# Soft stage of a graph network with a slice attention, x in triples: the row norm moved from VectorE to ScalarE, two tiles ahead, in eight slots

## The reference

```python
# graph part: x = x + MLP(layernorm(x), sums of the edge rows by their target row)
aggr = segment_sum(edge_features, edge_index[1], num_segments=6250)
h = relu(concat([layernorm(x), aggr]) @ W1 + b1)
x = x + relu(h @ W2 + b2) @ W3 + b3
# slice attention on the normed rows, 8 heads of 64, 64 slices each
xn = layernorm(x)
fx_mid, x_mid = heads(xn @ W_fx + b_fx), heads(xn @ W_x + b_x)
slice_weights = softmax((x_mid @ W_slice + b_slice) / clip(temperature, 0.1, 5), axis=-1)
slice_token = einsum('bhnc,bhng->bhgc', fx_mid, slice_weights) / (slice_weights.sum(rows) + 1e-5)
q, k, v = slice_token @ W_q, slice_token @ W_k, slice_token @ W_v
out_slice = softmax(q @ k.T / 8) @ v
x = x + (einsum of out_slice with slice_weights) @ W_out + b_out
```

## Time and profile before

| | us |
|---|---|
| median of 3 timed runs | 646.18 (644.64 to 648.68) |
| profiled execution, its own time | 645.15 |
| span of the profiled execution | 643.4 |
| PE busy | 600.5 (93%) |
| DVE busy | 389.9 (61%) |
| ACT busy | 281.8 (44%) |
| POOL busy | 231.3 (36%) |
| granted TensorE clock, mean | 0.991 |

### The profile page before, as it was taken

The page is one execution under the profiler, slowest core; times in us unless marked ns, Lnnn a source line. Parts: engine busy times, 40 slices in busy tenths (PEclk is TensorE's granted clock), DMA queues, the critical chain, the costliest instruction groups (busy, mean ns, idle before and its releaser), DMA issues.

```text
span 643.4 us, 11467 instructions
## 1 busy us (share of the span) xinstructions
PE 600.5 (93%) x3433; PEld 355.1 (55%) x3433; DVE 389.9 (61%) x1089; ACT 281.8 (44%) x400; POOL 231.3 (36%) x283
## 2 busy tenths in 40 slices
PE   5679999979998999999899899999999998999997
PEld 2345555544554555454489344444444444888885
DVE  6745545335576566655458888888888887322221
ACT  5145655612221222222120444555455546777772
POOL 4345565500000000000123666666666665595000
PEclk9799999989999999999999999999999999999999
DMA  8999999999999999996120134333343334011112
GB/s 296 380 396 397 408 409 408 373 350 386 366 361 384 377 353 369 385 362 251 41 81 1 33 66 77 70 65 65 68 77 68 65 66 81 25 73 73 73 73 81
DMA packets 104841, 134.01 MB, mean 208 GB/s; under 512 B 57339, under 2 KB 59345, under 8 KB 104805
## 3 DMA queue, kind: packets, MB, share of 16 engines
q1 hardware_dynamic: 103989, 133.29, 61.3%
q10 hardware_dynamic: 816, 0.26, 0.2%
HBM read 114.29 MB, written 6.40 MB: 188 GB/s over the span
## 4 chain that ended last, share of the span: by engine, by line
PE 74%; DMA 21%; DVE 2%; SPq 1%; issue 1%; ACT 0%; DVEq 0%
DMA ring_mem<-edge_attr_in 18%; PE ps L1583 13%; PE ps L1491 13%; PE ps L1515 13%; PE ps L1235 10%; PE ps L1356 7%; PE ps L1277 6%; PE ps L1271 5%; DMA x_sb<-x_in 3%; PE ps L1476 2%; PE ps L1266 2%; PE ps L1348 1%; SPq L404 1%; DVE ring_mem L1105 0%; DVE ring_mem L1107 0%
## 5 line engine op out<-in xcount | busy, mean ns | idle before, releaser
L969 DVE TENSOR_TENSOR big<-big,ps 128x64 f32 x319 | 70.6, 221 | 103.8 <-PE ps L1266 60.3
L1235 PE MATMUL ps<-ring_mem,side 128*32 128x256 f32 (+1 forms) x1596 | 103.2, 394 | 26.2 <-DMA ring_mem<-edge_attr_in 24.9
L1491 PE MATMUL ps<-ring_mem,xn 128*128 128x512 f32 x196 | 93.4, 599 | 1.0 <-DVE ring_mem L1119 0.7
L1515 PE MATMUL ps<-side,ring_mem 128*128 128x512 f32 x196 | 92.3, 593 | 1.9 <-ACT ring_mem L744 1.9
L1235 PEld LDWEIGHTS ps<-ring_mem,side 128*32 128x32 f32 (+1 forms) x1596 | 50.9, 112 | 63.9 <-issue 32.1
L1583 PE MATMUL ps<-side,ring_mem 128*128 128x256 f32 x360 | 77.9, 379 | 0.0
L640 POOL TENSOR_TENSOR ring_mem<-ring_mem 128x512 f32<-128x512 f32 x48 | 66.1, 1376 | 30.0 <-DVE ring_mem L1119 30.0
L1583 PEld LDWEIGHTS ps<-side,ring_mem 128*128 128x128 f32 x360 | 68.4, 190 | 9.3
L759 ACT ACTIVATE ring_mem<-ring_mem 128x512 f32<-128x512 f32 x49 | 30.9, 630 | 90.5 <-POOL ring_mem L633 90.5
L809 ACT ACTIVATE ring_mem<-big 128x1024 uint16 (+1 forms) x45 | 60.6, 1355 | 15.7 <-PE ps L1583 15.7
L603 POOL MEMSET ring_mem<- 128x128 f32 x1 | 0.2, 205 | 178.7 <-PE ps L1235 178.7
(11 more groups left out here) (136 smaller groups left out, 769.0 us busy)
## 6 DMA issues: line engine op xcount, KB each, us to landing
ring_mem<-edge_attr_in SPq DMA_DIRECT2D x84, 1024.0 KB, 8.9
ring_mem<-edge_attr_in SPq DMA_DIRECT2D x62, 256.0 KB, 5.0
x_sb<-x_in SPq DMA_DIRECT2D x16, 384.0 KB, 5.8
result<-x_sb SPq DMA_DIRECT2D x16, 384.0 KB
big<-side SPq DMA_TRANSPOSE x49, 3.1
side<-L_gnn_W_in SPq DMA_DIRECT2D x2, 256.0 KB, 6.5
ring_mem<-L_ffn_W_x_in SPq DMA_DIRECT2D x2, 256.0 KB, 3.7
ring_mem<-L_ffn_W_out_in SPq DMA_DIRECT2D x1, 512.0 KB, 3.8
```

Of the source, the lines that this page charges most:

```text
L969: dve.tensor_tensor(win, win, found[:, :, q * WINDOW:(q + 1) * WINDOW], ALU.add).then_inc(groups_added, 1)
L1235: return mm(ps[q * WINDOW:(q + 1) * WINDOW, SUM_BANKS[h], col:col + F], lhsT=hot[0:parts, h * 2 + j, t, :], rhs=ring8[0:parts, h * 2 + j, ...
L1491: last = mm(ps[:, 4 + k, :], lhsT=xn[:, r, k * P:(k + 1) * P], rhs=soft[:, r, :], start=isinstance(t, int) and t == 3, stop=isinstance(t, ...
L1515: last = mm(ps[:, s % 2, :], lhsT=xn_t[:, s % 2, k, :], rhs=wc[:, k, :], start=(k == 0), stop=(k == KF - 1))
```

## The change

`normalise` goes from DVE to ACT. ACT's instruction is an Identity activation with scale `rstd2` and bias `shift2` = -mean x rstd2, so POOL's `rstd` gets two more operations: a product of the mean with -1 (beside the addition) and, after the power, a product with it. They count up `pow2_ready` and `rstd2_ready`. ACT makes the rows of tiles 0, 1 and 2 before the first copy, and in its step t those of t+2, between the copy of xn_t and the exponential. At its step 1 it waits for POOL's last `rstd` step. The rows have eight slots: four in `xn` as before, four in columns 0 to 1023 of `ring_mem`. The steps of ACT, DVE and PE now run in a loop body of eight (`NORM_SLOTS`): eight steps written out in front, the loop four times on ACT and DVE and five times on PE, and the rest written out. PE's reads take the slot of the tile (`normed`). POOL and SP keep their body of four. The semaphore `pow2_ready` is new.

```diff
@@ -24,6 +24,8 @@
 P = 128
 UNROLL = 4
+NORM_SLOTS = 8
+NORM_AHEAD = 2
 WINDOW = 32
 CHUNK_GROUPS = 4
 ROWS_PER_PART = 2
...
@@ -91,17 +93,17 @@
         trip(i, 2 if i < TWOS // UNROLL else 4, P if i < FOURS // UNROLL else LAST_P, "x" if i < X_TRIPS else "")
 
-def run_steps(eng, step, total, peel_front, loop_trips):
-
-    first = peel_front * UNROLL
+def run_steps(eng, step, total, peel_front, loop_trips, unroll=UNROLL):
+
+    first = peel_front * unroll
     for t in range(first):
-        step(t, t % UNROLL, t // UNROLL)
+        step(t, t % unroll, t // unroll)
     with eng.Fori(peel_front, peel_front + loop_trips) as i:
-        for s in range(UNROLL):
-            step(i * UNROLL + s, s, i)
-    for t in range((peel_front + loop_trips) * UNROLL, total):
-        step(t, t % UNROLL, t // UNROLL)
+        for s in range(unroll):
+            step(i * unroll + s, s, i)
+    for t in range((peel_front + loop_trips) * unroll, total):
+        step(t, t % unroll, t // unroll)
 
 def build(nc, x, dst, edges, w1, b1, w2, b2, w3, b3, w_fx, b_fx, w_x, b_x, w_slice, b_slice,
...
@@ -195,6 +197,12 @@
         raw = part(1280, 256)
         tok = part(1536, 256)
         k_t = part(1792, 256)
+        more_xn = part(0, 1024).rearrange("p (b f) -> p b f", b=UNROLL)
+        def normed(s):
+            return xn[:, s, :] if s < UNROLL else more_xn[:, s - UNROLL, :]
         ones = part(7936, P // 2)
         att_mx = part(8000, 4)
         att_sm = part(8004, 4)
...
@@ -262,6 +270,7 @@
         mv2 = sb("mv2", [P, TILES, 2])
         eps = sb("eps", [P, X_TILES])
         rstd2 = part(4744, TILES)
+        shift2 = part(4744 + TILES, TILES)
         carrier = sb("carrier", [P, 1])
         mx, sm, rc = [part(8012 + n * UNROLL * H, UNROLL * H).rearrange("p (b h) -> p b h", h=H) for n in range(3)]
...
@@ -605,12 +615,15 @@
             def rstd(step, t, n, seen):
-                to = rstd2[:, bass.ds(t, n)]
+                to, shift = rstd2[:, bass.ds(t, n)], shift2[:, bass.ds(t, n)]
                 pool.wait_ge(mv2_ready, seen)
+                pool.tensor_tensor(shift, mv2[:, bass.ds(t, n), 0], minus[:, 0:1].broadcast_to([P, n]), ALU.mult)
                 pool.tensor_tensor(to, mv2[:, bass.ds(t, n), 1], eps[:, 0:1].broadcast_to([P, n]), ALU.add
                                    ).then_inc(var2_ready, 1)
                 pool.wait_ge(var2_ready, step + 1)
-                pool.tensor_tensor(to, to, half[:, 0:1].broadcast_to([P, n]), ALU.pow).then_inc(rstd2_ready, 1)
+                pool.tensor_tensor(to, to, half[:, 0:1].broadcast_to([P, n]), ALU.pow).then_inc(pow2_ready, 1)
+                pool.wait_ge(pow2_ready, step + 1)
+                pool.tensor_tensor(shift, shift, to, ALU.mult).then_inc(rstd2_ready, 1)
             FIRST = X_TILES * (L3_TRIPLES + 1)
             rstd(0, 0, FIRST, FIRST)
...
@@ -739,27 +752,44 @@
             relu_two(MLP_CHUNKS, P, [ps[:, 0, m * P:(m + 1) * P] for m in range(KF)])
 
+            def normalise(t, s):
+                if past(t, NORM_SLOTS):
+                    act.wait_ge(xn_used, t - NORM_SLOTS + 1)
+                act.activation(normed(s), of_tile(t), ACT.Identity, bias=shift2[:, bass.ds(t, 1)],
+                               scale=rstd2[:, bass.ds(t, 1)]).then_inc(xn2_ready, 1)
             def copy_xn_t(t, b):
                 act.wait_ge(tp_ready, t + 1)
                 act.activation(xn_t[:, b], ps[:, 2 + b, 0:2 * P].rearrange("p (k n) -> p k n", k=KF),
                                ACT.Copy).then_inc(xn_t_ready, 1)
+            def split(t, s, i):
+                act.wait_ge(sw_ready, t - 1)
+                if past(t, 4):
+                    act.wait_ge(turned[s % 2], (i * (NORM_SLOTS // 2) + s // 2 - 1) * 16)
+                act.activation(halves[:, s % 2], words(soft[:, (s - 2) % UNROLL, :]), ACT.Copy).then_inc(split_ready, 1)
             def soft_step(t, s, i):
+                b = s % UNROLL
                 if past(t, 2):
-                    act.wait_ge(sw_ready, t - 1)
-                    if past(t, 4):
-                        act.wait_ge(turned[s % 2], (i * 2 + s // 2 - 1) * 16)
-                    act.activation(halves[:, s % 2], words(soft[:, (s - 2) % UNROLL, :]), ACT.Copy).then_inc(split_ready, 1)
+                    split(t, s, i)
                 if before(t, TILES - 1):
                     if past(t, 1):
                         act.wait_ge(logits_ready, t)
                     copy_xn_t(t + 1, (s + 1) % 2)
+                if isinstance(t, int) and t == 1:
+                    act.wait_ge(rstd2_ready, RSTD_STEPS)
+                if past(t, 1) and before(t, TILES - NORM_AHEAD):
+                    normalise(t + NORM_AHEAD, (s + NORM_AHEAD) % NORM_SLOTS)
                 if before(t, TILES):
                     act.wait_ge(shifted, t + 1)
-                    act.activation(soft[:, s, :], soft[:, s, :], ACT.Exp).then_inc(exp_ready, 1)
+                    act.activation(soft[:, b, :], soft[:, b, :], ACT.Exp).then_inc(exp_ready, 1)
+            act.wait_ge(rstd2_ready, 1)
+            for t in range(NORM_AHEAD + 1):
+                normalise(t, t)
             copy_xn_t(0, 0)
-            run_steps(act, soft_step, TILES + 2, 2, (TILES - 1) // UNROLL - 2)
+            run_steps(act, soft_step, TILES + 2, 1, (TILES - 1) // NORM_SLOTS - 2, NORM_SLOTS)
             def merge_early(t):
                 act.activation(words(early[:, t, :]), sw_t[:, t], ACT.Copy).then_inc(staged, 1)
...
@@ -1085,26 +1115,17 @@
             full_residual(L3_TRIPLES + 6, 6)
 
-            def normalise(t, s):
-                if past(t, UNROLL):
-                    dve.wait_ge(xn_used, t - UNROLL + 1)
-                dve.tensor_scalar(xn[:, s, :], of_tile(t), mv2[:, bass.ds(t, 1), 0], rstd2[:, bass.ds(t, 1)],
-                                  ALU.subtract, ALU.mult).then_inc(xn2_ready, 1)
             def soft_step(t, s, i):
-                if isinstance(t, int) and t == 3:
-                    dve.wait_ge(rstd2_ready, RSTD_STEPS)
-                if past(t, 1) and before(t, TILES - 1):
-                    normalise(t + 1, (s + 1) % UNROLL)
                 if before(t, TILES):
                     dve.wait_ge(logits_ready, t + 1)
                     if past(t, UNROLL):
                         dve.wait_ge(split_ready, t - UNROLL + 1)
                         dve.wait_ge(xn_used, t - UNROLL + 1)
                         dve.wait_ge(sw_summed, t - UNROLL + 2)
-                    dve.tensor_tensor(soft[:, s, :], ps[:, s % 2, :], c_bc, ALU.add).then_inc(biased, 1)
+                    b = s % UNROLL
+                    dve.tensor_tensor(soft[:, b, :], ps[:, s % 2, :], c_bc, ALU.add).then_inc(biased, 1)
                     dve.wait_ge(biased, t + 1)
-                    dve.tensor_reduce(mx[:, s, :], heads(soft[:, s, :]), AX.X, ALU.max).then_inc(max_ready, 1)
+                    dve.tensor_reduce(mx[:, b, :], heads(soft[:, b, :]), AX.X, ALU.max).then_inc(max_ready, 1)
                 if past(t, 1):
                     r = (s - 1) % UNROLL
                     dve.wait_ge(exp_ready, t)
...
@@ -1128,7 +1146,7 @@
             residual(TRIPLES, TRIPLES - 1, X_TILES, 6)
             residual_stats(TRIPLES, TRIPLES - 1, X_TILES, TILES)
             dve.wait_ge(fold_v, 7)
-            run_steps(dve, soft_step, TILES + 1, 1, (TILES - 1) // UNROLL - 1)
+            run_steps(dve, soft_step, TILES + 1, 1, (TILES - 1) // NORM_SLOTS - 2, NORM_SLOTS)
 
             n_att = [0]
...
@@ -1473,7 +1491,7 @@
             def tp_rows(t, s):
                 pe.wait_ge(xn2_ready, t + 1)
                 for k in range(KF):
-                    last = tr(ps[:, 2 + s % 2, k * P:(k + 1) * P], xn[:, s, k * P:(k + 1) * P], ident[:, :])
+                    last = tr(ps[:, 2 + s % 2, k * P:(k + 1) * P], normed(s)[:, k * P:(k + 1) * P], ident[:, :])
                 last.then_inc(tp_ready, 1)
             def norms(of, first):
...
@@ -1486,9 +1504,10 @@
             def soft_step(t, s, i):
                 r = (s - 3) % UNROLL
+                rows = normed((s - 3) % NORM_SLOTS)
                 def token_sums(k):
-                    last = mm(ps[:, 4 + k, :], lhsT=xn[:, r, k * P:(k + 1) * P], rhs=soft[:, r, :],
+                    last = mm(ps[:, 4 + k, :], lhsT=rows[:, k * P:(k + 1) * P], rhs=soft[:, r, :],
                               start=isinstance(t, int) and t == 3, stop=isinstance(t, int) and t == TILES + 2)
                     if k == KF - 1:
                         last.then_inc(xn_used, 1)
...
@@ -1518,14 +1537,14 @@
                 if isinstance(t, int) and t == TILES - 1:
                     token_sums(1)
                 if before(t, TILES - 1):
-                    tp_rows(t + 1, (s + 1) % UNROLL)
+                    tp_rows(t + 1, (s + 1) % NORM_SLOTS)
 
             tp_rows(0, 0)
             pe.wait_ge(x2_ready, i + 8)
             full_layer3(TRIPLES - 1, 6)
             pe.wait_ge(fold_v, 7)
```

(6 more changed lines are left out.)

## The result

The changed kernel takes 639.12 us (median of 4 runs, 638.37 to 640.71) beside 646.42 us before (4 runs, 644.64 to 648.68): a ratio of 0.9889, with a 95% interval of 0.9864 to 0.9914. That is 7.3 us less where 6.1 were forecast, with bounds of 5.6 and 8.8 us from the interval. The median lies at 1.1%, just beyond the 1% line, and the interval holds the line.

A forecast was written before the change was run, and what follows sets the result against it. PE was taken as nearly full, losing a little to rows made just in time by DVE. Loop 5.2, five steps 0.3 and front 0.6 sum to 6.1 us less: 640.0 us given against 646.18, range 637.5 to 643.8.

The forecast's parts named there:

- The loop: Soft stage's loop of 40 tiles: 146.8 us instead of 152.0, 5.2 us less.
- The turns: Turns back of PE's soft-stage loop: four instead of nine, 0.1 us taken for each, between 0.3 us and nothing.
- full gain: Rival: turns back cost nothing and the front gives 0.8 us; 6.7 us less, 639.5 us; chance 0.28.
- DVE loses the normalisation: Soft-stage loop: DVE's 3.47 us a tile becomes 3.07, under PE's 3.66, so DVE isn't late any more.
- rows made a tile earlier: Soft-stage loop: PE's transposes no longer wait for their rows; 0.29 us go in four tiles.
- cost if cover were gone: ACT's norm, costed at nothing inside idle time; without that, up to 0.1 us in each of 46 tiles, 5 us.
- The five steps before the loop: Soft stage, 362.15 to 380.74 us: 18.30 us instead of 18.59, 0.3 us less.
- The front: Start of the soft stage: DVE's first L1105 starts 0.66 us earlier, first token sums follow; 0.6 us taken.
- the last rstd step: POOL, between its first and second subtraction: adds 0.4 us there; cost none, at worst 0.4 us once.
- The tail: Behind the last logits: DVE has no L1091 left there before either, so nothing changes.
- Slower by code fetch: Rival: eight-tile body exceeds what the sequencer holds, each turn fetches code, 3.1 us each; 655.5 us; chance 0.04.
- Half the gain: Rival: PE meets another just-in-time hand-over, likely the copy of xn_t, or turns keep 0.3 us; 642 to 644 us; chance 0.2.

The follow-up runs named there:

- e3_body_eight: The kernel before with loop bodies of eight tiles on ACT, DVE and PE, nothing else changed: 644.93 us, ratio 0.9971.
- e1_dve_ahead: The changed kernel with the row norm back on DVE, still two tiles ahead, eight slots and bodies of eight: 639.71 us, ratio 0.9913.
- e4_act_two_more: The changed kernel with two more activations of the norm's size on ACT behind each norm, into an unused buffer: 639.52 us in one execution.
- e2_four_slots: The changed kernel with four slots instead of eight, and so bodies of four tiles: 639.31 us, ratio 0.9895.
- e8_dve_four: The kernel before, norm still on DVE, but made two tiles ahead, between the reciprocal and the weights of tile t-1: 642.50 us, ratio 0.9938.
- e5_act_four_more: The changed kernel with four more activations of the norm's size on ACT behind each norm, into an unused buffer: 664.76 us in one execution.
- e7_act_one_ahead: The changed kernel with ACT making the rows one tile ahead, not two, between the split and the copy of xn_t: 675.31 us in one execution.

## Why the prediction was right, and where not

- *What bounds the kernel.* Right. PE loses its time to rows made just in time, and 3.66 us a tile was there to be had: 3.654. One reading was incomplete: the 0.19 us for which DVE was late at 403.35 came from DVE's own turn back (e3_body_eight), not only from its work.
- *The loop, 5.2 us forecast.* It gave 5.83. The turns, priced at 0.1 us each, cost nothing; that is 0.4 of the missing 0.6, and the rest is the clean step, 3.654 and not 3.66. The loop went as in the rival "full gain". The turns' price was taken in part from the loop of L1583, and that sum was low: 77.86 - 360 x 0.215 is 0.46 us for its ten turns, not 0.2; either is under 0.05 us a turn.
- *Cause of it.* The step "DVE loses the normalisation" was given as a reason and is none (e1_dve_ahead). The step "rows made a tile earlier" is all of it.
- *ACT.* Right: 1.25 us idle where about 1.2 was said, and the cover is real (e4_act_two_more). The forecast cost if cover were gone, up to 0.1 us a tile, was not tested by itself.
- *The five steps before the loop.* 0.22 us, 0.3 forecast.
- *The front, 0.6 us forecast.* This step failed: "It now starts at 355.6, 0.2 us behind the logits as in the loop and so 0.66 us earlier". The bias is as late as before, for the reason shown in the row of L950: I read that L1105 stood straight behind the statistics and didn't ask what the residual ahead of them waited for. Also the last rstd step wasn't free as said: POOL's subtraction of tile 1 fell further onto DVE's weights (1.28 us, 0.96 before), and the first token sums waited 0.15 us for them. What came is 0.41 us. Of it 0.21 are the transposes of tile 3, which don't wait for DVE's rows (363.37 - 361.55 = 1.82 us behind the logits' start, 361.87 - 359.84 = 2.03 before). The logits of tile 2 are 0.10 us sooner behind the transposes ahead of them, the first logits 0.12 behind theirs, and the token sums give 0.02 back.
- *The tail.* Right, 110.69 beside 110.66 us.
- *Sum.* 6.46 us in the traces beside 6.1. The errors of loop and front have opposite signs. The 7.3 us of the medians hold 0.8 more, which no trace places and the interval doesn't require.
- *Slower by code fetch.* Not seen in the changed kernel. Something like it was seen in DVE's longer body with the norm in it, once and for 1.1 us, under the 1.2 us at each turn that the rival needed. (By the code a tile has six matmul instructions, so PE's body grew from 24 to 48, not from 20 to 40.)
- *Half the gain.* The copy of xn_t was late 4 times, 1.0 us in all, covered.

## What to carry to other kernels

Where the bound engine waits a little at every step, ask how early its operand is made before asking which engine makes it: a lead of one more step gave all of the loop's 5.8 us, and moving the work without the lead cost 29.7. Work taken off an engine ahead of a wait is worth nothing if the wait ends when it did; follow the chain back to the instruction that waits for another engine. Where a prologue has the bound engine idle, put its own late work there.

## What the runs showed of the hardware

- A turn back of PE's loop cost 0.3 us where the rows came just in time (before, e3_body_eight), and nothing where they came earlier, with bodies of four (e2_four_slots, e8_dve_four) as of eight.
- Behind a turn back of DVE's loop the first bias started 0.39 us behind the transposes in before and 0.45 in the changed kernel and in e8_dve_four, where most other steps have 0.20. That cost a step of 0.19 us more in before, 0.13 in e8_dve_four and nothing in the changed kernel.
- DVE's first turn back with a body of eight tiles and the norm in it took 1.49 to 1.50 us for an instruction of 0.40, once, in e1_dve_ahead and e3_body_eight, and never with bodies of four. The page of both counts 18 packets on the instruction queue (q14), 16 in before and in e8_dve_four. But e5_act_four_more and e7_act_one_ahead count 18 too, without such an instruction on DVE or ACT, so the counts don't settle whether it is a fetch of code, and the cause stays open.
- DVE's weights (two operands in SBUF) take longer while POOL's subtraction runs. The rows of e8_dve_four, where they don't meet:

```profile
395.97 1.04 POOL L646 TENSOR_TENSOR ring_mem<-ring_mem 128x512 f32<-128x512 f32 x1 [0.58 <-DVE ring_mem L1121]
...
396.79 0.41 DVE L1108 TENSOR_SCALAR xn<-x_sb,mv,ring_mem 128x256 f32 x1
...
397.12 0.69 DVE L1137 TENSOR_TENSOR ring_mem<-ring_mem 128x512 f32<-128x512 f32 x1
```

  The weights take 0.69 us there, 0.80 in the changed kernel's loop, where they start 0.25 us before POOL's subtraction ends (365.85 against 365.06 + 1.04, in the rows of the front), and 1.28 where they start 0.72 us before (362.34 against 362.02 + 1.04). POOL's subtraction stays at 1.04 us: it is DVE that pays. POOL's sum of the weights took 1.38 us with DVE's norm beside it (L640 in before) and 1.28 without (L653).
